# First attention of a four-layer kernel: the router of a batch in three steps of the next batch but one, the final product in the fourth

## The reference

```python
def _L0_attn_a_ref(x, Mq, Mk, Mv):
    q = (x @ Mq).reshape(B, H, C, K)
    k = (x @ Mk).reshape(B, H, C, K)
    v = (x @ Mv).reshape(B, H, C, V)
    scores = jnp.einsum('bhqk,bhck->bhqc', q, k).reshape(B * H, C, C)
    att = jax.nn.softmax(scores / jnp.sqrt(jnp.float32(K)), axis=1)
    att4 = att.reshape(B, C, H, C)
    out = jnp.einsum('bqhc,bhcd->bqhd', att4, v)
    return out.reshape(B, C, H * V)

def _L0_ffn_ref(x, w_gate, b_gate, W1, b1, W2, b2):
    logits = x_flat @ w_gate + b_gate
    probs = jax.nn.softmax(logits, axis=-1)
    route_p = jnp.max(probs, axis=-1)
    route_idx = jnp.argmax(probs, axis=-1)
    h = jax.nn.relu(jnp.einsum('nd,edm->enm', x_flat, W1) + b1[:, None, :])
    y = jnp.einsum('enm,emd->end', h, W2) + b2[:, None, :]
    out = y[route_idx, jnp.arange(n)] * route_p[:, None]

x = x + _L0_attn_a_ref(_layernorm(x, axis=-1), ...)
x = x + _L0_ffn_ref(_layernorm(x, axis=-1), ...)
x = x + _L0_attn_b_ref(_layernorm(x, axis=-1), ...)
x = x + _L0_ffn_ref(_layernorm(x, axis=-1), ...)
```

## Time and profile before

| | |
|---|---|
| three runs, us | 568.34, 571.62, 572.99 |
| the profiled execution: time / span, us | 575.24 / 573.4 |
| its mean granted TensorE clock | 0.857 |
| busy: PE, DVE, ACT, POOL | 423.3, 324.9, 211.7, 202.3 us (74, 57, 37, 35% of the span) |
| the chain that ended last | PE 56%, DVE 15%, issue 8%, POOL 7%, ACT 7%, DMA 4% |

### The profile page before, as it was taken

How to read it: one execution, slowest core, us unless ns; L and a number is a source line. 1 busy time by engine, 2 the same in 40 slices (tenths; PEclk the granted TensorE clock), 3 DMA queues, 4 the chain that set the end, 5 groups by cost and what they waited for, 6 DMA issues and landing times.

```text
span 573.4 us, 14608 instructions
## 1 busy us (share of the span) xinstructions
PE 423.3 (74%) x4870; PEld 315.7 (55%) x4871; DVE 324.9 (57%) x1042; ACT 211.7 (37%) x483; POOL 202.3 (35%) x299
## 2 busy tenths in 40 slices
PE   2768878788872599955467899999888763999900
PEld 2646666666662377743135666766666652677800
DVE  2555656775666445426865576668776664444412
ACT  1445645544530022211135657655665400222200
POOL 3132335443445100027666335633612442000054
PEclk9968989998775699995567999999999955899965
DMA  8999200000000111111100000000000001111123
GB/s 271 348 337 296 83 2 13 11 5 5 10 11 27 29 55 53 50 38 37 27 0 2 1 2 3 0 0 0 1 2 10 29 19 32 39 53 54 41 70 90
DMA packets 40896, 30.91 MB, mean 54 GB/s; under 512 B 3344, under 2 KB 37008, under 8 KB 40592
## 3 DMA queue, kind: packets, MB, share of 16 engines
q1 hardware_dynamic: 32176, 23.06, 13.2%
q0 software_dynamic: 2048, 4.20, 2.5%
q10 hardware_dynamic: 6624, 3.02, 1.8%
HBM read 15.26 MB, written 15.01 MB: 53 GB/s over the span
## 4 chain that ended last, share of the span: by engine, by line
PE 56%; DVE 15%; issue 8%; POOL 7%; ACT 7%; DMA 4%; SPq 1%; ACTq 0%; DVEq 0%; POOLq 0%
PE S L1311 8%; PE bank L1324 7%; PE bank L1194 6%; POOL yg L1042 4%; PE S L1317 4%; PE S L1235 3%; PE S L1401 3%; ACT E L910 3%; PE bank L1354 3%; PE S L1402 2%; PE bank L1211 2%; DVE nmax L491 2%; PE bank L1414 2%; PE bank L1377 2%; PE bank L1154 2%
## 5 line engine op out<-in xcount | busy, mean ns | idle before, releaser
L829 ACT ACTIVATE E<-S,nmax 128x256 f32<-128x256 f32 x128 | 59.1, 478 | 59.7 <-DVE nmax L491 59.7
L1042 POOL DMA_INDIRECT yg<-slots,pos x32 | 30.8, 963 | 141.3 <-DMA slots<-yo 132.8
L872 ACT ACTIVATE hT<-S 128x512 f32<-128x512 f32 x46 | 27.5, 597 | 106.6 <-PE S L1317 106.6
L1003 POOL TENSOR_TENSOR vs<-Va,rden 128x512 f32<-128x512 f32 x32 | 33.3, 1040 | 80.1 <-DVE rden L520 77.2
L910 ACT ACTIVATE E<-S 128x1536 f32<-128x1536 f32 x32 | 46.4, 1450 | 25.7 <-PE S L1405 25.7
L1311 PE MATMUL S<-W,xgT 128*128 x92 | 52.3, 652 | 0.0
L677 DVE TENSOR_REDUCE nm<-bank 128x2 f32<-128x512 f32 x64 | 41.1, 684 | 16.1 <-PE bank L1377 16.1
L491 DVE TENSOR_REDUCE nmax<-S 128x4 f32<-128x1024 f32 x32 | 39.1, 1221 | 17.6 <-PE S L1235 16.6
L1324 PE MATMUL bank<-W,hT 128*128 x368 | 48.5, 276 | 0.0
L1324 PEld LDWEIGHTS bank<-W,hT 128*128 128x128 f32 x368 | 44.7, 192 | 0.1
L1148 PE MATMUL bank<-cst,xnb 128*128 128x128 f32 x44 | 11.9, 369 | 40.5 <-DVE xnb L415 29.6
(11 more groups left out here) (169 smaller groups left out, 1010.8 us busy)
## 6 DMA issues: line engine op xcount, KB each, us to landing
slots<-zeros SPq DMA_DIRECT2D x1, 8640.0 KB, 38.0
xg<-slots SPq DMA_DIRECT2D x46, 64.0 KB, 1.8
slots<-yo ACTq DMA_DIRECT2D x46, 64.0 KB, 1.6
W<-in_L_ffn_W SPq DMA_DIRECT2D x1, 2048.0 KB, 10.5
b<-in_L_ffn_b SPq DMA_DIRECT2D x1, 2048.0 KB, 20.1
x<-in_L_attn_a_x SPq DMA_DIRECT2D x4, 256.0 KB, 3.6
yg<-in_select SPq DMA_DIRECT2D x1, 1024.0 KB, 8.1
out<-x SPq DMA_DIRECT2D x8, 128.0 KB, 2.2
```

The costliest lines, as they stand in the source:

```text
L829: last = act.activation(E[:, hp, h, c, :], S[hp % 2][:, h, c * T:(c + 1) * T], ACT.Exp, bias=nmax[:, hp, k:k + 1], accum_out=den[:, hp, k: ...
L1042: pool.indirect_dma_start(out=yg[:, t, :], out_offset=None, in_=xs_dram, in_offset=bass.IndirectOffsetOnAxis(pos[:, t:t + 1], 0)).then_inc ...
```

## The change

In batch b, by step, for the router and the final product:

| | before | after |
|---|---|---|
| step 0 | `logits`, `route_logits` of b - 3 | `norm_apply`, transposes, `norm_out` of b - 2 |
| step 1 | `ranks`, `route_places`, scatter of b - 3 | `logits`, `route_logits` of b - 2 |
| step 2 | `a_final`, `a_add`, statistics and `inverse_deviation` of b - 1; `norm_apply` of b - 2 | `ranks`, `route_places` of b - 2 |
| step 3 | transposes, `norm_out` of b - 2 | `a_final`, `a_add`, statistics of b - 1; on GpSimd scatter of b - 2, `inverse_deviation` of b - 1, then `vs` |

`OT` gets a second set, so that the final product of a batch may come when the next batch's first two `OT` are already written. The router's `wg` and `bg` are counted on the semaphore `b_loaded`, since batch 2 now needs them. Behind the loop the router of batch 5 is gone from the tail. GpSimd clears `sofar` and `keys` only when the table is there. In the first step of the expert tiles TensorE transposes the second tile behind the first tile's product and not ahead of it.

The buffer:

```diff
-        OT = sb("OT", [P, 2, 2, 4, RT])
+        OT = sb("OT", [P, 2, 2, 2, 4, RT])
```

VectorE, `a_step`:

```diff
-                if hp == 2 and lag:
-                    a_add(b - 1)
                 if hp >= 2 or lag:
-                    a_outT(g - 2, (hp + 2) % 4)
+                    a_outT(g - 2, (hp + 2) % 4, p if hp >= 2 else 1 - p)
...
-                if hp == 0 and there(b - 3):
-                    route_logits(0, b - 3, 1 - p, pb[3])
-                if hp == 1:
-                    if there(b - 3): route_places(0, b - 3, 1 - p, pb[3])
-                if hp == 2:
-                    if there(b - 1): dve.wait_ge(a_x, b)
-                    if there(b - 2): norm_apply(1, b - 2, p)
-                    if there(b - 1):
-                        norm_stats(1, b - 1, 1 - p)
+                if hp == 0 and there(b - 2):
+                    norm_apply(1, b - 2, p)
+                if hp == 1 and there(b - 2):
+                    route_logits(0, b - 2, p, pb[3])
+                if hp == 2 and there(b - 2):
+                    route_places(0, b - 2, p, pb[3])
+                if hp == 3 and lag:
+                    a_add(b - 1)
+                if hp == 3 and there(b - 1):
+                    dve.wait_ge(a_x, b)
+                    dve.sem_inc(norm[1]["go"], 1)
+                    norm_stats(1, b - 1, 1 - p)
```

ScalarE, `a_step`:

```diff
-                if hp == 3 and there(b - 2):
+                if hp == 0 and there(b - 2):
                     norm_out(1, b - 2, p, pb[3])
```

GpSimd, `a_batch` and what stands behind it:

```diff
+                    if hp == 3 and there(b - 2):
...
+                        scatter(0, b - 2, p)
+                    if hp == 3 and there(b - 1):
+                        inverse_deviation(1, b - 1, 1 - p)
                     a_values(b * 4 + hp, hp, p, lag)
-                    if hp == 1 and there(b - 3):
-                        scatter(0, b - 3, 1 - p)
-                    if hp == 2 and there(b - 1):
-                        inverse_deviation(1, b - 1, 1 - p)
...
-            scatter(0, 5, 1)
...
+            pool.wait_ge(ffn[0]["table"], 1)
+            pool.memset(sofar[:, :], 0.0).then_inc(pool_const, 1)
             pool.wait_ge(a_scores, 4 * B)
             pool.memset(keys[:, :], 0.0).then_inc(bs["zero"], 1)
-            pool.wait_ge(ffn[0]["totals"], 1)
-            pool.memset(sofar[:, :], 0.0).then_inc(pool_const, 1)
```

TensorE, `a_step`:

```diff
-                if hp == 0 and there(b - 3): logits(0, b - 3, 1 - p, pb[3])
-                if hp == 1 and there(b - 3): ranks(0, b - 3, pb[3])
-                if hp == 3 and there(b - 2):
-                    pe.wait_ge(a_x, b)
-                    norm_transpose(1, b - 2, p, pb[3])
                 if nxt and hp < 3:
                     a_project(b + 1, 1 - p, hp, True)
-                if hp == 2 and lag:
-                    if there(b - 3):
-                        pe.wait_ge(ffn[0]["pos"], b - 2)
...
-                    a_final(b - 1)
...
+                if hp == 0 and there(b - 2):
+                    pe.wait_ge(a_x, b - 1)
+                    norm_transpose(1, b - 2, p, pb[3])
+                if hp == 1 and there(b - 2): logits(0, b - 2, p, pb[3])
+                if hp == 2 and there(b - 2): ranks(0, b - 2, pb[3])
+                if hp == 3 and lag:
+                    if there(b - 2):
+                        pe.wait_ge(ffn[0]["pos"], b - 1)
...
+                    a_final(b - 1, 1 - p)
```

## The result

| | before | after |
|---|---|---|
| median, us (four runs each, in turn on one chip) | 571.71 (568.34 to 572.99) | 588.51 (583.83 to 589.82) |
| profiled execution: time / span, us | 575.24 / 573.4 | 587.94 / 586.1 |
| mean granted TensorE clock | 0.857 | 0.845 |

The account below looks back on a forecast made before the run. TensorE was taken to lead in busy time and in the chain that ended last. The terms 1.1 + 1.7 + 6.5 - 2.6 = +6.7 us on 571.6 gave 578.3 us, range 569 to 586.

Parts of the forecast that it names:

- The cycle: Attention loop, batches 3 to 7: a chain through GpSimd sets the period at 17.8 us against 17.4, +1.1 us.
- x: The moment in a batch when TensorE's transposes behind `norm_apply` are done; the next was forecast 17.8 us later.
- Batch 2 to 3: Batch 2 newly routes batch 0, so batch 3's step 1 scores come later: +1.7 us.
- The clock: Holes ahead of the transposes in batches 3 to 7 lower TensorE's clock, 1.3 us each: +6.5 us.
- the case of my sum: Slow stretches of about 3.4 us at half speed behind the holes, priced at 1.3 us each; chance 0.47.
- the last rival: Two or three longer slow stretches in the loop, 3 to 5 us each: +15, about 587 us; chance 0.16.
- Tail: Behind the loop: batch 5's `route` leaves, batch 7's steps get longer; put at 0, bounds -1 and +1.5 us.
- Memset: Behind the attention: clearing `keys` after the table frees VectorE's `expert`, -2.6 us, bounds -2.6 and -3.5.
- First-tile order: Expert tiles: first matmul ahead of the second tile's transpose, -0.1 to -0.3 us, lost in rounding.

Follow-up runs that it names:

- e4: The changed kernel with nine unused 128x128 matmuls on TensorE ahead of the step 0 transposes, batches 3 to 7: 574.84 us, ratio 1.0064.
- e13: The kernel before with four overwritten 128x128 matmuls ahead of `logits` in step 0 of batches 3 to 7: 570.5 us, ratio 0.9935.
- e15: The changed kernel itself, unchanged, run on the third chip: 588.01 us, ratio 1.0236.
- e11: The kernel before with the two memsets behind the table and four overwritten matmuls ahead of `logits` in step 0, batches 3 to 7: 567.01 us, ratio 0.9911.
- e2: The kernel before with only the memsets of `sofar` and `keys` moved behind the table: 570.03 us, ratio 0.998.
- e3: The kernel before with only the second expert tile's transpose moved behind the first tile's product: 573.14 us, ratio 1.0041.
- e10: The changed kernel with inverse deviation ahead of the scatter and the first expert tile order as before, third chip: 582.59 us, ratio 1.017.
- e12: The changed kernel with GpSimd's step 3 order inverse deviation, `vs`, scatter, and the first expert tile order as before: 570.69 us, ratio 0.9981.
- e14: Same as e12 plus four unused matmuls ahead of the step 0 transposes, batches 3 to 7: 566.98 us, ratio 0.9848.
- e5: The changed kernel with the first expert tile order as before: 584.62 us, ratio 1.0159.
- e9: The changed kernel with inverse deviation ahead of the scatter, run on the third chip: 587.88 us, ratio 1.0287.
- e7: The changed kernel with four unused matmuls ahead of the step 0 transposes, batches 3 to 7: 580.16 us, ratio 1.011.
- e1: The changed kernel with inverse deviation ahead of the scatter in GpSimd's step 3, first chip: 571.13 us, ratio 0.9971.

## Why the prediction was right and wrong

- **The cycle: right.** `norm_apply` in step 0 waits for `rstd`, which stands behind the `vs` of step 2 and a scatter in GpSimd's queue; the next x is x + 17.8. e4 shows it bare (17.81, 17.81, 17.82, then 17.39 for the forecast 17.4), so the term **+1.1** was measured as +1.1 (70.83 for 69.71). That it fits to 0.02 us is in part luck: by e4's rows `rstd` was there at x+15.6 and not x+15.4, and from there to the next x it took 2.2 us and not 2.4. And the 69.71 holds a slow stretch of its own; against the kernel before with its clock up (e13, 68.2) the cycle costs 2.6 us. Its parts are there too: places 0.94 us under `vs` (forecast 0.17 + 0.6, bounds 0 and 0.9), the pair of `norm_apply` under `vs` and `xb` 1.65 us (forecast 1.86, bounds 0.6 and 1.9). Both collisions were of the kind that the Trainium skill (SBUF — State Buffer, section "Who interferes with whom") gives to whoever issues second, and here, other than at 165.22 in the earlier trace rows, the trace agrees: `vs` had started 0.13 and 0.14 us earlier (91.48 and 91.61, 99.54 and 99.68).
- **Batch 2 to 3: right.** +1.4 for +1.7.
- **The clock: the step that failed.** The step reads "The clock. [...] Five such holes (before x in batches 3 to 7), each at 0 to 1.7 (3.4 us at half speed); I take 1.3 each: +6.5". That it falls at each of the five holes, within 2 us of the transposes, was right. The length was not. I took the one stretch of 3.4 us behind the 2.11 us hole as the length of all, and made the upper bound from it. Behind the 3.3 us holes the stretches were 6.8 us, and over 13 us in batch 7. A stretch of 6.8 us spans transposes (0.66 for 0.41 us), scores (2.08 for 1.13) and K projection (3.41 for 1.97), which are all on the cycle: 2.6 us by these rows, 20.5 - 17.8 = 2.7 by the periods, twice my 1.3. Batch 3 (3.4 us long, about 2.0) and e15, the same kernel on a chip where the clock fell in every other batch (3.4 us long, 1.6 each), show the case of my sum. What makes a stretch 3.4 or 6.8 us long stays open. The Trainium skill (TensorE: Matmul & The Clock Gate, section "Terms") puts the loss at about the slow time times one minus the granted share, 3.4 us for 6.8 and 1.7 for 3.4; the runs agree from below, 2.7 and 1.6, since part of the slow time covered TensorE's idle time. All in all the term was 12.8 us by e4 (10.0 in the loop, 2.4 in batch 7, 0.5 behind it) against 6.5: this alone is most of the miss, and the last rival ("the slow stretches last") was the one that came true, with its mechanism spread over most batches, 2.7 us each, rather than 3 to 5 in two or three.
- **Tail: right as a sum, by two parts that cancel.** With the clock up through most of batch 7 (until 165.7 in e4, until 157.0 in e11, which stands for the kernel before) the stretch from its step 1 scores takes 15.1 us for 13.4, +1.7, and the stretch to the first expert tile, without batch 5's router, 20.7 for 21.8, -1.2. Against the trace of before, where the clock was at 0.5 for 10.2 us, e4's 15.1 stands beside 15.4 (-0.3); the +2.1 of the change, slow in both, is batch 7's longer steps and a longer slow stretch together.
- **Memset: right.** -2.6 in e2's trace (forecast -2.6), -3.3 in the change for the whole stretch up to the first tile, in which batch 5's router is missing too.
- **First-tile order: wrong sign.** Forecast -0.1 to -0.3, "lost in rounding"; measured +1.1 in e3. I had moved the instruction on TensorE and not asked in what order VectorE takes what TensorE makes.

I had also misread the trace of before. Its hole of 2.11 us was not the longest of the loop: one of 2.34 us stands at 96.13, in the window 84 to 102 of the earlier trace rows, and the clock stayed at 1.00 behind it. So that trace already showed that the length of a hole does not settle what the clock does.

```profile
96.13 0.61 PE L1154 MATMUL bank<-wg,xnTb 128*128 128x8 f32 x4 [2.34 <-ACT xnTb L811]
```

The terms as measured, 1.4 + 1.1 + 12.8 - 0.3 - 3.3 + 2.5 (the two expert stretches of the trace), make +14.2. For the two traces, which differ by 12.7, take off 0.65 (before batch 2), 0.44 (middle) and the 0.5 that stands both in the clock and in the -3.3: 12.6. By the medians it is 14.2 in e15 and 16.8 in the first measurement; that difference is not explained. Kernels that share the code of the middle of the program, between the two expert mixtures, also differ there by over 5 us from trace to trace (231.0 in e11, 236.4 in e14).

## What to carry to other kernels

When a change gathers scattered idle time of TensorE into one hole, take as upper bound of the clock's price all the critical work right behind the hole at half speed (here 4.1 us a batch, of which 1.6 to 2.7 came true), and not the length of the slow stretches that the old trace happens to show; then try a few useless matmuls in the hole, since they are the cheapest test of whether the clock is the cause, and here were also worth 0.7% to the kernel before, though they did not hold it every time (e11). When a consumer is moved a whole batch closer to its producer, walk through the in-order queue of every engine between the two: here a scatter that nobody waits for stood ahead of the one value that everybody waited for, and putting it last took the same idea from 1.017 to 0.998 on one chip (e10, e12). Before calling the idea a gain, give its helps to the old kernel too: with them it was as fast (e11, e14). An edit in one engine's order needs the matching edit in the engine that consumes it.

## What the runs showed of the hardware

- The length of a hole alone gives neither whether the granted clock falls nor for how long. It stayed at 1.00 behind 2.34 us in the kernel before and fell to 0.50 for 3.4 us behind 2.11 us there; behind holes of 2.1 us it fell for 6.8 us in two batches of e5 and not at all in two of e15; behind 3.3 us it fell for 6.8 us, behind the 3.8 to 4.0 us of e9 mostly for 3.4. With four matmuls in the hole and 1.0 to 1.3 us of idle time left it stayed up in the loops of e7 and e13 and fell once in e11.
- One program (e1, e9) took 0.997 of the kernel before on one chip and 1.029 on another, with all executions of each chip on its own side (564.3 to 572.7, 583.9 to 590.0). The traces part where VectorE copies the values while GpSimd issues a scatter: the copy waits 1.9 to 2.3 us in three batches of e9. Two of these (119.49 and 140.34) fall where the trace has no instruction fetch (111 to 155 us), so the loading of code is not it. What lies behind it stays open.
- TensorE's block of 32 matmuls without a wait stopped on its way in several traces, with no releaser in the profile: for 0.7 us in all in e15 (first after the 20th), for 1.25 us in the change's own trace, once, in the block that starts at 60.56.
